# Routed tokens transposed by block exchange and VectorE in place of TensorE, and low weights made in two parts on two tiles

## The chip, the cores and the metric

The kernel runs on one core of a Trainium2 chip. The metric is device time in microseconds (us), the median of three runs of one launch. On the engines: PE (TensorE, with its weight loads as PEld), DVE (VectorE), ACT (ScalarE), POOL (GpSimd) and SP (SyncE, here an issuer of DMAs). Each engine has a sequencer that works through its instructions in order: waits, register loads from SBUF, branches and DMA issues are done there, and in rows they carry a q (PEldq).

## The reference, cut to what matters

A Mamba layer (a selective scan over 4 batches of 512 tokens) gated by the normed x is added to x; then a mixture of experts is added to that:

```python
x = x + tanh(g_xattn[0]) * mamba(ctx_1024, layernorm(x), ...)
h = layernorm(x)                              # 2048 tokens x 512
scores = softmax(h @ gate_w.T)                # 16 experts
topk_w, topk_ids = top_k(scores, 6)           # then made to sum to 1, as combine
for e in range(16):                           # hidden size I = 352
    g, u = split(h @ w13[e].T); acc += combine[:, e] * ((silu(g) * u) @ w2[e].T)
out = acc + shared(h)                         # the same form, hidden size 2 * 352
x = x + tanh(g_ffn[0]) * out
```

All of it is float32.

## The kernel before, in words

The first third of the span is stage A, the scan. Behind it stand 136 tiles of 128 tokens each (TILES). Tiles 0 to 31 (NS = 32) are the shared part, twice the 16 token tiles, with the shared weights as two sets; tiles 32 to 135 are routed. Each expert's tokens are listed and cut into tiles of 128, and a table in SBUF, `meta`, holds for each tile its expert, where its weights lie, whether it is the first or the last of an expert, and its column in the lists. Engines read it by register loads (`value_load`), since the plan depends on the data.

A matmul in single precision is made of three: each operand is split into a rounded high part and the low rest, and high x high, high x low and low x high are added. So a tile needs x_high (ACT, L852) and x_low (DVE, L1363); PE's `up`, 24 matmuls (L1699, L1700); ACT's silu and DVE's `multiply`; PE's `turn_a`, three transposes (L1710); ACT's a_high (L862) and DVE's a_low (L1399); PE's `down`, nine matmuls (L1719); ACT's y_out (L868); and POOL's add into the output, an indirect DMA with accumulation (L1015). PE's order in tile t is: half of up(t), turn_a(t - 1), the other half, turn_x(t + 1), down(t - 1), so that ACT and DVE have time between.

Routed x comes to its tile by POOL's indirect gather (L997) of 128 rows of `rows_d`, a table in DRAM of all tokens' rows with their routing weights behind; it is issued five tiles ahead (AHEAD) into `xt`, with four slots. A gathered tile has tokens on partitions, and `up` wants features there, so PE transposes it in four 128x128 pieces into bank 4 (turn_x, L1687), from which x_high and x_low read. DVE copies the routing weights of a tile (take_weight, L1372) and the row numbers of gather and add (L1378, L1383), each behind a register load (L1369, L1375).

Weights of an expert are one DMA of 2176 KB into `wraw`, issued by SP (L633). ACT (L822) and DVE (L1417) cast half of the high parts each on the tile ahead of the expert's first, and POOL makes all the low parts with one subtraction (L987). `w` holds two experts, so that PE changes between them by an offset, which it loads for each tile (weights_of, L1724 and L1726).

The order on each engine is written out: shared tiles and the first routed ones are unrolled, and from there each engine has a loop of four tiles. `apart` is a semaphore wait with a register's value. SP stores the rows of a batch into `rows_d` (L609) as soon as they are normed.

Of the kernel before, what the change touches and what calls it, by code (L numbers as in the profile page):

```python
# [64 lines left out]
AHEAD = 5  # L65
FIRST_ROWS = {NS - 3: (NS, NS + 1), NS - 2: (NS + 2,), NS - 1: (NS + 3, NS + 4)}
# [100 lines left out]
               8: [("exp", 3)], TT - 3: [("fetch", 2)]}  # L167
# [64 lines left out]
def mamba_moe(nc, x, ctxT, g_x, g_f, inT, convw, convb, xpT, dtwT, dtb, alog, dvec,  # L232
# [12 lines left out]
    with ExitStack() as ctx:  # L245
# [113 lines left out]
        wraw = alloc(ctx, "wraw", [P, WCOLS])  # L359
        w = alloc(ctx, "w", [P, 4 * WCOLS], F32R)  # L360
# [5 lines left out]
        cc = alloc(ctx, "cc", [P, 2])  # L366
# [8 lines left out]
        meta = alloc(ctx, "meta", [P, 5, NT], I32)  # L375
# [13 lines left out]
        fours = alloc(ctx, "fours", [P, 2], I32)  # L389
# [57 lines left out]
        gathered = [sem(f"gathered{i}") for i in range(4)]  # L447
        zero_done = sem("zero_done")
# [16 lines left out]
        cc_done = sem("cc_done")  # L465
# [42 lines left out]
        def routed_groups(eng):  # L508

            return eng.value_load(fours[0:1, 0:1], min_val=E // 4, max_val=ROUTED // 4)  # L510

# [29 lines left out]
        def _(sp):  # L541
# [42 lines left out]
            def step(b, at):  # L584
# [7 lines left out]
                if b == NB - 1 and n == 2:  # L592
                    sp.wait_ge(dA_done, b * DS * J)
                    sp.wait_ge(g_done, b * DS)
                    sp.wait_ge(summed, (b - 1) * DS * J + J * J)
                    fetch(0)
# [10 lines left out]
            def rows(b, _):  # L607
                sp.wait_ge(norm_done, TC * (b + 1))
                sp.dma_start(rows_v[b, :, :, 0:H + 2], rowb[:]).then_inc(rows_stored, 16)  # L609
# [20 lines left out]
            def fetch(e):  # L630

                at_least(sp, wl_done, e)
                sp.dma_start(wraw[:], wall[bass.ds(e, 1)].rearrange("a p c -> p (a c)")).then_inc(raw_in, 16)  # L633
# [24 lines left out]
            with sp.Fori(3, NX) as e:  # L658
                fetch(e)
            sp.wait_ge(meta_ready, 2)  # L660
            tiles = tiles_but_12(sp) + 12
# [5 lines left out]
        def _(act):  # L667
# [92 lines left out]
            def norm_chunk(b, t):  # L760
                act.wait_ge(nmr2_done, b + 1)
                act.wait_ge(rows_stored, 16 * (b + 1))
# [53 lines left out]
            def split_high(e, t):  # L816


                mine = WCOLS - SHARE
                apart(act, raw_in, 16 * (e + 1), "act")  # L820
                apart(act, down_done, t, "act")
                nc.scalar.copy(columns(w, (e % 2) * 2 * WCOLS, mine), wraw[:, 0:mine]).then_inc(wh_done, 1)  # L822
# [14 lines left out]
            def fetch(e):  # L837

                act.wait_ge(wl_done, e)
                act.dma_start(wraw[:], wall[bass.ds(e, 1)].rearrange("a p c -> p (a c)")).then_inc(raw_in, 16)  # L840
# [40 lines left out]
            def high_piece(e, k):  # L881
# [5 lines left out]
                nc.scalar.copy(w[:, base + at:base + at + size], wraw[:, at:at + size]).then_inc(*split(e, k, EARLY))  # L887
# [51 lines left out]
        def _(pool):  # L939
# [43 lines left out]
            def split_low(e):  # L983

                at = (e % 2) * 2 * WCOLS
                apart(pool, wh_done, 2 * (e + 1), "pool")
                nc.gpsimd.tensor_tensor(columns(w, at + WCOLS, WCOLS), wraw[:], columns(w, at, WCOLS), ALU.subtract).then_inc(wl_done, 1)  # L987

            def gather(t, s):

                if isinstance(t, int) and t < NS + 4:
                    pool.wait_ge(xl_done, t - 3)
                else:
                    apart(pool, xt_turned, t - 3, "pool")
                    apart(pool, cc_done, t - 3, "pool")
                apart(pool, gid_done, t + 1, "pool")
                pool.indirect_dma_start(xt[:, s, :], None, rows_d[:, :],  # L997
# [47 lines left out]
            for t in range(NS):  # L1045
                if t == NS - 3:
                    pool.wait_ge(wts_stored, 16 * NB)
                    pool.wait_ge(rows_stored, 16 * (NB + 1))
                for late in FIRST_ROWS.get(t, ()):
                    gather(late, late % 4)  # L1050
# [12 lines left out]
            with pool.Fori(0, groups - 2) as i:  # L1063
                for k in range(4):
                    t = 4 * i + NS + k
                    gather(t + AHEAD, (k + AHEAD) % 4)
# [4 lines left out]
            for k in range(8):  # L1071
                if k + AHEAD < 8:
                    gather(rest + k + AHEAD, (k + AHEAD) % 4)
# [6 lines left out]
        def _(dve):  # L1080
# [226 lines left out]
            def count_tiles(half):  # L1307

                if half:
# [5 lines left out]
                    chained(nc.vector.tensor_scalar(fours[:, 0:1], fours[:, 0:1], -float(NS // 4), None, ALU.add))  # L1315
                    return
# [26 lines left out]
            def fill_table(half):  # L1343
                if half == 0:
# [10 lines left out]
                                                       op0=ALU.is_lt, op1=ALU.mult))  # L1355
                nc.vector.scalar_tensor_tensor(out=meta[:, 2, :], in0=slot[:], scalar=1.0, in1=fresh[:],
# [8 lines left out]
            def take_weight(t, s4, m=None):  # L1365
# [3 lines left out]
                e = dve.value_load(meta[0:1, 0, bass.ds(t, 1)], min_val=1, max_val=NX)  # L1369
                rows_in(dve, t, s4, m, "dve")  # L1370
                at_least(dve, am_done, t - 1)
                nc.vector.tensor_copy(cc[:, s4 % 2:s4 % 2 + 1], xt[:, s4, bass.ds(H - 1 + e, 1)]).then_inc(cc_done, 1)  # L1372
# [4 lines left out]
            def gather_ids(t, s4):  # L1377
# [7 lines left out]
            def multiply(t, s):  # L1385
# [3 lines left out]
                else:  # L1389
                    dve.wait_ge(cc_done, t + 1)  # L1390
                    weight = cc[:, s:s + 1]
# [9 lines left out]
            def low_piece(e, k):  # L1401
# [4 lines left out]
                low = nc.vector.tensor_tensor(w[:, base + WCOLS + at:base + WCOLS + at + size], wraw[:, at:at + size],  # L1406
# [4 lines left out]
            def next_weights(t):  # L1411

                e = dve.value_load(meta[0:1, 2, bass.ds(t, 1)], min_val=0, max_val=NX - 1)
                with dve.If(e > 0):
                    apart(dve, raw_in, 16 * (e + 1), "dve")
# [405 lines left out]
```

## Time and profile before

| | |
|---|---|
| median of three runs | 1436.62 us (1435.21 to 1438.37) |
| the profiled execution: its span (the records show no time of its own beside it) | 1435.5 us |
| PE busy, of the span | 1349.9 us, 94% |
| POOL, DVE, ACT busy | 66%, 55%, 51% |
| DMA moved | 149.13 MB, mean 104 GB/s |
| granted TensorE clock, 720 to 1400 us | 1.00 (2.4 GHz) |

A busy share is a mean over stages; in the routed part DVE, ACT and POOL are far from full and PE nearly is. Matmuls' ends are modelled, so a busy PE need not be PE at its peak. An idle time is given with what ended it; "issue" is idle time that no wait in the profile explains, in which an engine's sequencer was still at something else.

### The profile page before, as it was taken

Reading aid. Unit: us, or ns where it says so; the run is one execution under the profiler, and the core shown is the slowest. Engines: PE = TensorE matmul, PEld = TensorE weight load, DVE = VectorE, ACT = ScalarE, POOL = GpSimd, SP = SyncE. Lnnn points to the kernel's source line nnn. Section 1 sums busy time; section 2 is a strip of 40 time slices with the busy share of each in tenths; the row PEclk is TensorE's granted clock in tenths of the full one; section 3 lists DMA queues with packets and bytes.
Section 4 is the critical chain, followed back from the end, with each engine's and each line's share of the span. In section 5 each row is a group of like instructions: output and inputs, shape, how many; then the busy total and the mean of one; then the engine's idle time right before and its main releaser. Section 6 shows DMA issues by size and latency. Waiting matters only on the chain.

```text
span 1435.5 us, 32257 instructions
## 1 busy us (share of the span) xinstructions
PE 1349.9 (94%) x8480; PEld 1210.6 (84%) x8481; DVE 787.5 (55%) x1364; ACT 730.9 (51%) x1317; POOL 949.3 (66%) x671
## 2 busy tenths in 40 slices
PE   6897998997898899999999999999999999999996
PEld 2686887887888799999998989989889988899885
DVE  6878898898989854653333333333333333333331
ACT  5898897898889464343332333323333333332321
POOL 0588898898988747887456665566645666546632
PEclk8899999999999999999999999999999999999999
DMA  4120122222242365645455435555445544454432
GB/s 137 38 74 31 53 67 96 67 73 91 75 146 72 133 129 106 142 84 141 83 141 145 131 63 144 139 147 137 104 94 137 141 135 104 95 147 131 76 68 36
DMA packets 65042, 149.13 MB, mean 104 GB/s; under 512 B 16976, under 2 KB 17616, under 8 KB 62656
## 3 DMA queue, kind: packets, MB, share of 16 engines
q0 software_dynamic: 31024, 62.10, 22.9%
q1 hardware_dynamic: 33392, 81.21, 17.5%
q10 hardware_dynamic: 560, 4.98, 1.0%
q8 instruction: 36, 0.59, 0.2%
q14 instruction: 30, 0.25, 0.1%
HBM read 101.50 MB, written 48.99 MB: 105 GB/s over the span
## 4 chain that ended last, share of the span: by engine, by line
PE 65%; DVE 3%; issue 1%; POOL 0%; ACT 0%; DVEq 0%; POOLq 0%; ACTq 0%
PE bank L1719 19%; PE bank L1699 19%; PE bank L1700 18%; PE bank L1687 3%; PE bank L1710 3%; DVE hs L1172 1%; PE bank L1604 1%; PE bank L1590 1%; PE bank L1602 0%; POOL hc L949 0%; DVE sc L1226 0%; PE bank L1665 0%; DVEq L1375 0%; DVE xl L1363 0%; DVE du L1186 0%
## 5 line engine op out<-in xcount | busy, mean ns | idle before, releaser
L949 POOL TENSOR_TENSOR hc<-hs,crow 128x512 f32<-128x512 f32 x254 | 322.6, 1302 | 91.8 <-DVE hs L1172 84.6
L1699 PE MATMUL bank<-w,xh 128*128 (+1 forms) x1088 | 368.7, 340 | 7.6 <-issue 4.2
L1015 POOL DMA_INDIRECT out_x<-ys,aid x104 | 171.2, 1646 | 275.0 <-issue 215.7
L1700 PE MATMUL bank<-w,xh 128*128 (+1 forms) x1088 | 351.2, 323 | 0.0
L1172 DVE TENSOR_TENSOR_SCAN hs<-dA,bank 128x512 f32<-128x512 f32 x256 | 295.8, 1208 | 47.9 <-PE bank L1604 32.0
L1719 PE MATMUL bank<-w,ah 128*128 (+1 forms) x816 | 264.7, 405 | 2.7 <-DVE al L1399 2.7
L1399 DVE TENSOR_TENSOR al<-bank,ah 128x384 fp32r<-128x384 f32 x136 | 75.8, 557 | 331.0 <-ACT ah L862 283.2
L1699 PEld LDWEIGHTS bank<-w,xh 128*128 128x128 f32 x1088 | 204.3, 188 | 35.9 <-issue 32.1
L1700 PEld LDWEIGHTS bank<-w,xh 128*128 128x128 f32 x1088 | 206.4, 190 | 2.3
L868 ACT COPY ys<-bank 128x512 f32<-128x512 f32 x136 | 79.9, 587 | 195.9 <-PE bank L1719 191.5
L1700 PE MATMUL bank<-w,xl 128*128 (+1 forms) x544 | 175.9, 323 | 0.0
L1699 PE MATMUL bank<-w,xl 128*128 (+1 forms) x544 | 175.7, 323 | 0.0
L1719 PEld LDWEIGHTS bank<-w,ah 128*128 128x128 f32 x816 | 145.0, 189 | 27.7 <-issue 2.2
L1590 PE MATMUL bank<-ident,hc 128*128 128x128 f32 x1024 | 160.4, 281 | 7.6 <-POOL hc L949 5.1
L862 ACT CAST ah<-bank 128x384 fp32r<-128x384 f32 x136 | 65.3, 480 | 196.9 <-PE bank L1710 166.7
L786 ACT ACTIVATE dA<-delta,aneg 128x512 f32<-128x512 f32 x256 | 164.0, 710 | 0.0
L1604 PE MATMUL bank<-bdiag,duT 128*128 128x128 f32 x1024 | 163.7, 285 | 0.0
L1719 PE MATMUL bank<-w,al 128*128 (+1 forms) x408 | 161.2, 395 | 0.0
L852 ACT CAST xh<-bank 128x512 fp32r<-128x512 f32 x104 | 61.2, 588 | 182.9 <-PE bank L1687 175.4
L987 POOL TENSOR_TENSOR w<-wraw,w 128x4352 f32 x15 | 143.8, 9588 | 0.7 <-issue 0.5
L1604 PEld LDWEIGHTS bank<-bdiag,duT 128*128 128x128 f32 x1024 | 142.5, 201 | 0.0
L1590 PEld LDWEIGHTS bank<-ident,hc 128*128 128x128 f32 x1024 | 124.3, 145 | 11.0 <-POOL hc L949 6.7
(184 smaller groups left out, 2051.7 us busy)
## 6 DMA issues: line engine op xcount, KB each, us to landing
wraw<-in_wall SPq DMA_DIRECT2D x16, 2176.0 KB
crow<-c_rows SPq DMA_DIRECT2D x64, 256.0 KB, 3.3
xt<-token_rows_turned SPq DMA_DIRECT2D x32, 256.0 KB
out_x<-ys POOLq DMA_DIRECT2D x32, 256.0 KB
wraw<-in_wall ACTq DMA_DIRECT2D x2, 2176.0 KB
token_rows<-rowb SPq DMA_DIRECT2D x4, 1028.0 KB
xrow<-in_x SPq DMA_DIRECT2D x4, 1024.0 KB, 7.0
out_x<-xrow SPq DMA_DIRECT2D x4, 1024.0 KB, 4.9
```

The source lines that it names most:

```text
L786: nc.scalar.activation(dA[:, 4 * (n % 2) + j, :], delta[b % 2][:, j, :], ACT.Exp, scale=aneg[:, j, n:n + 1]).then_inc(dA_done, 1)
L868: nc.scalar.copy(ys[:, slot, :], banks[7][:]).then_inc(ys_done, 1)
L949: nc.gpsimd.tensor_tensor(hc[:, j, :], hs[:, j, :], crow[:, n % 4, :], ALU.mult).then_inc(hc_done, 1)
L987: nc.gpsimd.tensor_tensor(columns(w, at + WCOLS, WCOLS), wraw[:], columns(w, at, WCOLS), ALU.subtract).then_inc(wl_done, 1)
L1015: pool.indirect_dma_start(out_rows, bass.IndirectOffsetOnAxis(ap=aid[:, s:s + 1], axis=0), ys[:, s, :], None, bounds_check=TOKENS - 1, oob ...
L1172: nc.vector.tensor_tensor_scan(hs[:, j, :], dA[:, 4 * (n % 2) + j, :], dbu[j % 2][:], 0.0, ALU.mult, ALU.add).then_inc(scanned, 1)
L1399: nc.vector.tensor_tensor(al[:, s, :], banks[5][:, 0:IP], ah[:, s, :], ALU.subtract).then_inc(al_done, 1)
L1590: mm = nc.tensor.matmul(ysum[t][:, cols], hc[:, j, t * P:(t + 1) * P], ident[:], start=n == 0 and j == 0, stop=n == DS - 1, is_transpose=T ...
L1604: mm = nc.tensor.matmul(dbu[j % 2][:, t * P:(t + 1) * P], duT[b % 2][:, t, j * P:(j + 1) * P], bdiag[:, n % 2, t - COPIED, :], start=True, ...
L1699: nc.tensor.matmul(gate_bank[:, 0:I], xx, columns(w, off + ww + k * 2 * I, I), start=first, stop=last)
L1700: mm = nc.tensor.matmul(up_bank[:, 0:I], xx, columns(w, off + ww + k * 2 * I + I, I), start=first, stop=last)
L1719: mm = nc.tensor.matmul(banks[7][:], aa, columns(w, off + ww + W2AT + k * H, H), start=k == 0 and n == 0, stop=k == IK - 1 and n == 2)
```

## The change

- `turn_x` is gone from PE. SP exchanges blocks instead: a gathered pair of tiles (`rowg`, four slots) is copied by 16 DMAs, each 32 partitions x 2 tiles x 512 bytes, so that block (q, c) of 32 partitions goes to block (c, q) of `xq` (part of `wraw`). DVE's `turn`, one instruction that transposes within 32x32 blocks, writes the whole turned tile into bank 4, at the start of DVE's tile, ahead of a_low. So that this is a transposition, a row's columns are stored in `rows_d` in another order: SP's store becomes 17 DMAs a batch in place of one.
- Gathers go out eight tiles ahead in place of five, row numbers seven, and routing weights three in place of one. The first row numbers are copied at tile 28 (with the wait for the lists), not 29.
- SP no longer fetches weights. ACT issues the fetch, at the last tile of an expert by a new column of `meta`, into `wnext` with two buffers, one expert further ahead.
- POOL makes the low weights in two instructions of half the width, the first on the tile it was on, the second on the next, by another column of `meta`: one more register load a tile on POOL, and one on ACT.

The diff, cut to its core:

```diff
+QUAD = P // 32
+AHEAD = 8
+TAKEN = 3
+FIRST_IDS = {NS - 4: (NS, NS + 1, NS + 2, NS + 3), NS - 2: (NS + 4, NS + 5), NS - 1: (NS + 6,)}
...
+            def exchange(i, h):
+                for k in (2 * h, 2 * h + 1):
+                    apart(sp, gathered[k], 16 * i + 16, "sp")
+                apart(sp, xt_turned, 4 * i + NS + 2 * h - 2, "sp")
+                for q in range(QUAD):
+                    for c in range(QUAD):
+                        sp.dma_start(xq[32 * c:32 * c + 32, 2 * h:2 * h + 2, q * P:(q + 1) * P],
+                                     rowg[32 * q:32 * q + 32, 2 * h:2 * h + 2, c * P:(c + 1) * P]).then_inc(swapped[h], 16)
...
+                last = act.value_load(meta[0:1, 5, bass.ds(t, 1)], min_val=0, max_val=NX - 2)
+                with act.If(last > 0):
+                    apart(act, wl_done, last, "act")
+                    fetch(last + 1)
...
-            def gather(t, s):
+            def gather(t, s, m):
+                if not (isinstance(m, int) and m == 0):
+                    apart(pool, swapped[s // 2], 16 * QUAD * QUAD * m, "pool")
                     apart(pool, cc_done, t - 3, "pool")
                 apart(pool, gid_done, t + 1, "pool")
...
+                before = pool.value_load(meta[0:1, 6, bass.ds(t, 1)], min_val=0, max_val=NX - 1)
+                with pool.If(before > 0):
+                    split_low(before, 1)
                 e = pool.value_load(meta[0:1, 2, bass.ds(t, 1)], min_val=0, max_val=NX - 1)
                 with pool.If(e > 0):
-                    split_low(e)
+                    split_low(e, 0)
...
+            def turn(t, s4, m):
+                apart(dve, swapped[s4 // 2], 16 * QUAD * QUAD * (m + 1), "dve")
+                dve.wait_ge(xh_done, t)
+                dve.wait_ge(xl_done, t)
+                nc.vector.transpose(banks[4][:].rearrange("p (k q j) -> p q k j", k=HK, q=QUAD),
+                                    xq[:, s4, :].rearrange("p (q k i) -> p q k i", q=QUAD, k=HK)).then_inc(xt_turned, 1)
...
+            def tile(t, s4, m=0, gathers=False, takes=False, adds=False):
+                turn(t + 1, (s4 + 1) % 4, m + (s4 + 1) // 4)
                 a_low(t - 1, 1 - s)
...
                 up(t, s, (2, 3), off)
-                if more and not (isinstance(t, int) and t + 1 < NS):
-                    turn_x(t + 1, (s4 + 1) % 4, m)
                 down(t - 1, 1 - s, old() if callable(old) else old)
```

On PE, before, in the routed loop, from the end of up to the register loads of the next tile:

```order
L1700 MATMUL bank<-w,xl 128x352
L1687 MATMUL bank<-ident,xt 128x128 [waits gathered1,xl_done]
L1687 MATMUL bank<-ident,xt 128x128 x3
L1719 ISA [waits ys_done,al_done]
L1719 MATMUL bank<-w,ah 128x512
...
L1719 MATMUL bank<-w,al 128x512
L1724 ISA
L1724 TENSOR_LOAD meta
```

The same place after (at the end of a group of four, so with the loop's branch):

```order
L1772 MATMUL bank<-w,xl 128x352
L1791 ISA [waits ys_done,al_done]
L1791 MATMUL bank<-w,ah 128x512
...
L1791 MATMUL bank<-w,al 128x512
L1828 REGISTER_ALU
L1828 COMPARE_AND_BRANCH
...
L1796 TENSOR_LOAD meta
```

The transposes and their waits are gone; the register load still stands behind all of down.

On DVE, before, the start of a routed tile:

```order
L1399 TENSOR_TENSOR al<-bank,ah 128x384 [waits down_done,ah_done]
L1369 ISA
L1369 TENSOR_LOAD meta
L1369 ISA x2
L1372 ISA [waits gathered1,am_done]
L1372 COPY cc<-xt 128x1
```

After:

```order
L1436 STREAM_TRANSPOSE bank<-wraw 128x4x4x32 [waits swapped0,xl_done,xh_done]
L1468 TENSOR_TENSOR al<-bank,ah 128x384 [waits down_done,ah_done]
L1424 ISA
L1424 TENSOR_LOAD meta
L1424 ISA x2
L1427 ISA [waits gathered3,am_done]
L1427 COPY cc<-rowg 128x1
```

The turn stands ahead of a_low, with its wait for the exchange (`swapped0`).

On POOL, before, a routed tile from its gather to its add:

```order
L997 DMA xt<-token_rows,gid 128x532 [waits gid_done]
L1032 ISA
L1032 TENSOR_LOAD meta
...
L987 TENSOR_TENSOR w<-wraw,w 128x4352
L1033 UNCONDITIONAL_BRANCH
L1038 ISA
L1038 TENSOR_LOAD meta
...
L1015 DMA out_x<-ys,aid 2048x512 [waits ys_done,aid_done]
```

After:

```order
L497 REGISTER_ALU [waits swapped0]
L497 REGISTER_ALU [waits cc_done]
L1045 DMA rowg<-token_rows,gid 128x532 [waits gid_done]
L1080 ISA
L1080 TENSOR_LOAD meta
...
L1035 TENSOR_TENSOR w<-wnext,w 128x2176
...
L1083 TENSOR_LOAD meta
...
L1035 TENSOR_TENSOR w<-wnext,w 128x2176
...
L1089 TENSOR_LOAD meta
```

The gather waits for the exchange, and three register loads stand where two did.

## Rows read from the trace of the kernel before

**Rows 1.** Page: busy us, share and count; two groups: busy, mean ns.

```profile
PE 1349.9 (94%) x8480; PEld 1210.6 (84%) x8481; DVE 787.5 (55%) x1364; ACT 730.9 (51%) x1317; POOL 949.3 (66%) x671
...
L1172 DVE TENSOR_TENSOR_SCAN hs<-dA,bank 128x512 f32<-128x512 f32 x256 | 295.8, 1208 | 47.9 <-PE bank L1604 32.0
...
L987 POOL TENSOR_TENSOR w<-wraw,w 128x4352 f32 x15 | 143.8, 9588 | 0.7 <-issue 0.5
```

**Rows 2.** Windows: us, then PE, PEld, DVE, ACT, POOL busy; clock, DMA share, GB/s.

```profile
720.00:1400.00 680.00, 673.70 (x3931) 612.66 (x3930) 241.73 (x603) 225.53 (x407) 394.83 (x212) 1.00 0.49 120
```

**Rows 3.** Chain of waits from 720 to 1400 us, by line.

```profile
by line: PE bank L1719 29.4%; PE bank L1699 29.1%; PE bank L1700 27.5%; PE bank L1687 6.1%; PE bank L1710 4.7%; issue 1.8%; DVEq L1375 0.4%; DVE xl L1363 0.3%; DVEq L1369 0.2%; ACT ah L862 0.2%; ACTq L872 0.1%; DVEq L487 0.0%; DVE al L1399 
```

**Rows 4.** Page, costliest groups: weight loads of L1699; behind the bar, idle before.

```profile
L1699 PEld LDWEIGHTS bank<-w,xh 128*128 128x128 f32 x1088 | 204.3, 188 | 35.9 <-issue 32.1
```

**Rows 5.** Timeline of weight loads at tile starts: start us, us, instruction, [idle before].

```profile
899.93 0.19 PEld L1699 LDWEIGHTS bank<-w,xh 128*128 128x128 f32 x1
...
906.67 0.19 PEld L1699 LDWEIGHTS bank<-w,xh 128*128 128x128 f32 x1
...
1003.45 0.19 PEld L1699 LDWEIGHTS bank<-w,xh 128*128 128x128 f32 x1 [0.18 <-issue]
...
1010.48 0.19 PEld L1699 LDWEIGHTS bank<-w,xh 128*128 128x128 f32 x1 [0.45 <-issue]
...
1017.18 0.19 PEld L1699 LDWEIGHTS bank<-w,xh 128*128 128x128 f32 x1
```

**Rows 6.** Timeline of DVE, a_low and the gather ids.

```profile
1006.54 0.56 DVE L1399 TENSOR_TENSOR al<-bank,ah 128x384 fp32r<-128x384 f32 x1 [2.24 <-ACT ah L862]
...
1008.52 0.15 DVE L1378 COPY gid<-lists 128x1 int32 x1 [0.86 <-issue]
...
1021.25 0.56 DVE L1399 TENSOR_TENSOR al<-bank,ah 128x384 fp32r<-128x384 f32 x1 [1.23 <-ACT ah L862]
```

**Rows 7.** Register loads of L1724: ns min/median/max, first and last start us.

```profile
L1724 PEldq TENSOR_LOAD <-meta x103: 296/385/1000, 703.9 to 1411.3; - x103
...
L1724 PEldq TENSOR_LOAD <-meta x1: 897/897/897, 1008.0 to 1008.0; - x1
...
L1724 PEldq TENSOR_LOAD <-meta x1: 298/298/298, 1023.1 to 1023.1; - x1
```

**Rows 8.** Timeline of POOL, adds.

```profile
1005.61 1.59 POOL L1015 DMA_INDIRECT out_x<-ys,aid  x1 [4.11 <-issue]
...
1019.35 2.13 POOL L1015 DMA_INDIRECT out_x<-ys,aid  x1 [4.12 <-ACT ys L868]
```

**Rows 9.** Timeline of ACT, y_out of tile 31 and of tile 134.

```profile
706.65 0.59 ACT L868 COPY ys<-bank 128x512 f32<-128x512 f32 x1 [1.38 <-PE bank L1719]
...
1419.97 0.59 ACT L868 COPY ys<-bank 128x512 f32<-128x512 f32 x1 [1.79 <-PE bank L1719]
```

**Rows 10.** DVE by line, 900 to 1400 us: busy, mean ns, idle before, releasers.

```profile
L1363 DVE TENSOR_TENSOR xl<-bank,xh 128x512 fp32r<-128x512 f32 x72 | 49.8, 692 | 15.6 <-ACT xh L852 14.4
...
L1399 DVE TENSOR_TENSOR al<-bank,ah 128x384 fp32r<-128x384 f32 x72 | 40.1, 557 | 171.2 <-ACT ah L862 148.7 <-issue 22.5
```

**Rows 11.** Timeline of SP's queue, two DMA issues one behind the other.

```profile
24.61 0.43 SPq L628 DMA_DIRECT2D ids<-in_ids_d  x1
25.09 0.43 SPq L628 DMA_DIRECT2D tri<-in_tri_d  x1
```

**Rows 12.** Timelines at 676 to 685 us, and the lists' DMA (KB, us to landing).

```profile
676.40 0.56 DVE L1399 TENSOR_TENSOR al<-bank,ah 128x384 fp32r<-128x384 f32 x1 [3.79 <-issue]
...
677.62 0.63 PE L1719 MATMUL bank<-w,ah 128*128 128x512 f32 x2
...
678.11 0.59 POOL L1060 DMA_DIRECT2D lists<-token_lists  x1 [0.47 <-DMA token_lists<-ids,posi]
...
lists<-token_lists POOLq DMA_DIRECT2D x1, 136.0 KB, 3.8
...
684.58 0.15 DVE L1378 COPY gid<-lists 128x1 int32 x1 [0.60 <-issue]
```

More of the change, by code:

```diff
@@ L447, in mamba_moe @@
         gathered = [sem(f"gathered{i}") for i in range(4)]
+        swapped = [sem(f"swapped{i}") for i in range(2)]
+        cc_done = sem("cc_done")
         zero_done = sem("zero_done")
@@ L608, in rows @@
                 sp.wait_ge(norm_done, TC * (b + 1))
-                sp.dma_start(rows_v[b, :, :, 0:H + 2], rowb[:]).then_inc(rows_stored, 16)
+                with nc.allow_non_contiguous_dma(reason="a row's columns by quadrant of the transposed row"):
+                    for t in range(TC):
+                        for c in range(QUAD):
+                            sp.dma_start(rows_v[b, :, t, c * P:(c + 1) * P].rearrange("p (k i) -> p k i", k=HK),
+                                         rowb[:, t, 0:H].rearrange("p (k c i) -> p c k i", k=HK, c=QUAD)[:, c]).then_inc(rows_stored, 16)
+                    sp.dma_start(rows_v[b, :, :, H:H + 2], rowb[:, :, H:H + 2]).then_inc(rows_stored, 16)
             def turned_(b, _):
@@ L657, in _ @@
                 x_load(t)
-            with sp.Fori(3, NX) as e:
-                fetch(e)
-            sp.wait_ge(meta_ready, 2)
+            def exchange(i, h):
[3 more added lines that the diff above has]
+                for q in range(QUAD):
+                    for c in range(QUAD):
+                        sp.dma_start(xq[32 * c:32 * c + 32, 2 * h:2 * h + 2, q * P:(q + 1) * P],
+                                     rowg[32 * q:32 * q + 32, 2 * h:2 * h + 2, c * P:(c + 1) * P]).then_inc(swapped[h], 16)
+            sp.wait_ge(meta_ready, 2)
+            sp.wait_ge(wl_done, 2)
+            groups = routed_groups(sp)
+            with sp.Fori(0, groups) as i:
+                for h in range(2):
+                    exchange(i, h)
             tiles = tiles_but_12(sp) + 12
@@ L1489, in _ @@
             groups = routed_groups(dve)
-            tile(PEELED, PEELED % 4)
+            tile(PEELED, PEELED % 4, -1)
             next_weights(PEELED)
-            for k in range(1, 4):
-                tile(PEELED + k, (PEELED + k) % 4, True, True)
-                next_weights(PEELED + k)
-            with dve.Fori(0, groups - 1) as i:
+            for t in range(NS, NS + 3):
+                tile(t, t % 4, 0, gathers=True, takes=True, adds=True)
+                next_weights(t)
+            most = groups_but_2(dve)
+            with dve.Fori(0, most) as i:
                 for k in range(4):
                     t = 4 * i + NS + 3 + k
-                    tile(t, (3 + k) % 4, True, True, i + 1)
+                    tile(t, (3 + k) % 4, i + (3 + k) // 4, gathers=True, takes=True, adds=True)
                     next_weights(t)
-            last = tiles_but_12(dve) + 11
-            a_low(last - 1, 0)
-            add_ids(last, 3)
-            multiply(last, 1)
-            a_low(last, 1)
+            rest = tiles_but_12(dve) + 7
+            for k in range(4):
+                tile(rest + k, (3 + k) % 4, most + (3 + k) // 4, takes=k < 2, adds=True)
+                next_weights(rest + k)
+            a_low(rest + 3, 0)
+            add_ids(rest + 4, 3)
+            multiply(rest + 4, 3, most + 1)
+            a_low(rest + 4, 1)
         @block.tensor
@@ L1681, in beside @@
                         last_count(i)
-            def turn_x(t, s, m=None):
-                rows_in(pe, t, s, m, "pe")
-                at_least(pe, xl_done, t)
-                for k in range(HK):
-                    mm = nc.tensor.transpose(banks[4][:, k * P:(k + 1) * P], xt[:, s, k * P:(k + 1) * P], ident[:])
-                mm.then_inc(xt_turned, 1)
             def up(t, s, chunks, off):
@@ L1726, in weights_of, with tile @@
                 return pe.value_load(meta[0:1, 1, bass.ds(t, 1)], min_val=0, max_val=2 * WCOLS)
-            def tile(t, s4, old, off, more=True, m=None):
+            def tile(t, s4, old, off):
                 s = s4 % 2
@@ L1764, in _ @@
                     off = weights_of(4 * i + PEELED + k)
-                    tile(4 * i + PEELED + k, (3 + k) % 4, old, off, True, i)
+                    tile(4 * i + PEELED + k, (3 + k) % 4, old, off)
                     old = off
@@ L1770, in of_last @@
                 return pe.value_load(meta[0:1, 1, bass.ds(last - k, 1)], min_val=0, max_val=2 * WCOLS)
-            tile(last, 3, lambda: of_last(1), weights_of(last), False)
+            tile(last, 3, lambda: of_last(1), weights_of(last))
             turn_a(last, 1)
```

129 lines of the change are left out of this document (77 added, 52 removed).

## The prediction

> **What bounds the kernel now.** I read the page's busy shares first, then the table of windows, the chain of waits, the costliest groups, and the timelines of single tiles. Two statements about the routed part are both true and lead to different forecasts. PE is busy 94% of the span [rows 1] and 673.7 of 680 us between 720 and 1400 us [rows 2], and the chain of that stretch is nearly all matmuls, 6.1% of it the x transposes of L1687 [rows 3]: 41.5 us for 98 tiles, 0.42 a tile. Read alone, that says: take 104 x 0.42 us away and the time falls by as much. But the ends of matmuls are modelled, and the weight loads tell another story: ahead of L1699, PEld stood idle 35.9 us in all, 32.1 of it put down to issue [rows 4]. Something holds PE's sequencer at the start of many tiles while the array has nothing to do.
>
> The timeline of one tile shows it. It begins with its first weight load at 1003.45, and the next at 1010.48, after 0.45 us of idle [rows 5]: 7.03 us. VectorE's a_low (L1399), which the down matmuls need, ends at 1006.54 + 0.56 = 1007.10 [rows 6], 3.65 after the start. The sequencer is held at the first down matmul until then, issues the nine, and only then reaches the register load of the next tile's weights (L1724), which starts at 1008.0, 0.90 later, and takes 0.897 [rows 7]. From its end at 1008.90 to the next tile's start lie 1.58 us, in which the second load (L1726) stands. 3.65 + 0.90 + 0.90 + 1.58 = 7.03: the tile is this chain, and the x transposes are not in it.
>
> The load is not always so long: 103 of them took 0.296 at least, 0.385 in the median, 1.000 at most [rows 7], and 0.485 as the mean that I work out over the 103. The long ones follow the add of a finished tile (L1015): add at 1005.61 [rows 8], load at 1008.0, 2.4 behind it, ended 3.3 behind it. Where the add lay further back, at 1019.35 [rows 8], 3.75 ahead of the load at 1023.1, the load took 0.298 [rows 7]. In the loads that I looked at, those that start 2 to 3 us behind an add end about 3.3 behind it, and others are short. I call them held.
>
> Without a held load the chain has 3.64 + 0.92 + 0.30 + 1.53 = 6.39 us, each the value that its piece has in most of the 103 tiles. Every fourth tile has 0.40 more at the loop's end (a_low's end at 1021.25 + 0.56, [rows 6], the load at 1023.1: 1.3 in place of 0.9): 6.49 in the mean. Where no load is held the array decides: 899.93 to 906.67, 6.74, without issue idle at either end [rows 5]. So now a tile takes the longer of the two.
>
> From the y_out of tile 31 at 706.65 to the next to last at 1419.97 [rows 9] are 103 tiles in 713.3 us, 6.93 each. 15 of them change the expert (15 low-weight instructions, [rows 1]); there the casts stand ahead of a_high and a_low, as in the tile from 1017.18 [rows 5], whose a_low ends at 1021.81, 4.63 after the start. That is 0.9 more than elsewhere in the mean of nine that I read, and 0.13 over all tiles. The chain's account of now: 6.49 + 0.19 held + 0.13 casts = 6.81; the 0.12 that is missing to 6.93 is what the array adds where it is the longer one.
>
> **The change, part by part.**
>
> *The transposes go from PE.* The array's floor falls to 6.74 - 0.42 = 6.3, below the chain's 6.49. What is late next is therefore the chain alone: if loads are held as now and the casts stay, 6.81 against 6.93, 0.12 x 103 = 12 us gained.
>
> The Trainium skill bears on the price of the load. On the page DMA: Bandwidth & Descriptors, section Latency and other measured facts, it gives tensor_load a floor of about 600 ns. By that the chain would have 0.3 more than it has here, the array's fall would bring nothing, and the sum would be 12 us higher. The measured 0.296 decides, and the sum does not use the page.
>
> *VectorE's turn comes in.* One 128x512 transpose per tile, ahead of a_low. No row shows one: the nearest are x_low, 0.692 on the same shape [rows 10], and the scan, 1.208 [rows 1]; I take 0.7. In 72 tiles a_low waited 171.2 us, 148.7 of it for ScalarE's a_high [rows 10], 2.1 a tile: either end fits in. Cost 0; if the turn came late and that cover were gone, each 0.1 us is 10 us. x_high and x_low are ready earlier, off the chain: no gain.
>
> *The exchange on SP.* Sixteen DMAs for a pair of tiles. SP's issues stand 0.48 us apart (24.61, 25.09, [rows 11]), and a load of 136 KB landed 3.8 after issue [rows 12]: 16 x 0.48 + 3.8 = 11.5 us, against 13.8 for two tiles, and it starts a tile and a half before the pair is over. It reads and writes 0.5 MB more in 13.8 us, 38 GB/s. The 16 DMA engines are busy 0.49 of the time at 120 GB/s [rows 2]; by bytes that is 0.16 more. Cost 0; the bound above is a pair that takes longer than two tiles, a rival below. The stores of the rows, 17 in place of one for each batch, lie beside a scan that doesn't wait for them: 0.
>
> *Weights earlier and issued by ScalarE; low weights in halves.* PE does not wait for low weights (9.59 us, [rows 1], against six or seven tiles between experts); two parts of 4.8 change nothing there. ScalarE gets one more load and branch a tile, an estimated 0.8 us on an engine busy a third of the time [rows 2]: 0. But POOL's gather, now for tile t + 8 where it was t + 5, waits for gather ids that VectorE copies a tile later, and POOL's register loads, three where there were two, stand behind it and ahead of the add. The ids end 5.2 after a tile's start (1008.52 + 0.15, [rows 6]). The gather's issue and three loads with their branches, estimated by VectorE's 0.75 from one load's copy to the next [rows 12], make 8.2, and the add 1.0 behind them comes 9.2 after that start, 2.5 after the next one; now it is 2.16 (1005.61 - 1003.45). PE's first load, 4.56 after the start, is then 2.06 behind the add, at the edge of the stretch in which it is held; in even tiles, in which the gather also waits for the exchange, it lies elsewhere. Bounds: no load held, 0, or one held in full in each tile, 0.70. I take as much as now, 0.19.
>
> *The start of the routed part.* VectorE now waits for the token lists ahead of tile 28 in place of tile 29. The lists' DMA is issued at 678.11 and lands 3.8 later, at 681.9, where a_low of tile 27 ran at 676.40 [rows 12]. Behind the wait stands that a_low, and PE's down matmuls, now at 677.62 [rows 12], wait for it: a_low ends at 682.5, and PE loses about 5.0. Then four gather-id copies stand ahead of x_low, where there were two, 0.15 + 0.60 each (684.58, [rows 12]): 1.5 more. With 1 us for the four operations added at tile 20 and the three takes at tile 31: 7.5 us lost. The bounds are 0, if the lists came 5 us earlier, and 12.
>
> **Sum.** On the profiled execution: 1435.5 - 12 + 7.5 = 1431.0. The records show its span only, which is 1.1 below the median of the three timed runs, 1436.6. So 1432 us, 0.3% less.
>
> **Rivals.**
>
> *The array is the bound.* For it: 99% busy, and the chain of waits [rows 2, 3]. Against it: 32.1 us of issue idle [rows 4] and the sum of 7.03. It gives 44 less and 7.5 more: 1400.
>
> *No load is held any more.* For it: the moved add is near the edge, and PE's load may miss the stretch in most tiles. Against: the add moves differently in even tiles. 0.12 + 0.19 = 0.31 x 103 = 32: 1436.6 - 32 + 7.5 = 1412.
>
> *Slower: a load is held in each tile.* The moved add puts one of PE's two loads, of L1724 or of L1726, into the stretch in every tile. For it: the tile shown, held 0.6 us, and two loads that can be hit; against: while POOL makes low weights no add is out, and that is now in two tiles of each six or seven. 6.49 + 0.70 + 0.13 = 7.32: 0.39 x 103 = 40 and 7.5, 1484; if it holds half of the tiles, 6.97, 1448. It decides from 0.24 us of holding a tile on, where the gain falls below the 7.5 of the start.
>
> *Slower: the exchange sets the pace.* It does so from 13.8 / 16 = 0.86 us per DMA on. At 1.0 a pair takes 16 us: 2.2 x 52 = 114 us, 1558. Against: issues 0.48 apart [rows 11], if their landings overlap.
>
> In the Trainium skill the page DMA: Bandwidth & Descriptors, section Rules for kernel authors, speaks for this one: many small transfers should be made one, since under 64 KB one pays mostly overhead; a DMA of the exchange has 32 KB. The trace shows small loads issued one behind the other without such a pause.
>
> **Chances.** The forecast, the chain with loads held about as now: 0.45, with its own range of 1422 to 1443. Array 0.10; no load held 0.17; a load held in each or in half of the tiles 0.22; exchange 0.06. A measurement of this kernel tells 0.2%, 2.9 us, from no change. Faster: 0.10 + 0.17 and 0.21 of the forecast's, 0.48; same: 0.15 of the forecast's and 0.03 of the half-held case, 0.18; slower: 0.19 + 0.06 and 0.09 of the forecast's, 0.34. The range leaves out the fully held case, the exchange, and the lower edge of the array's: 1397 to 1460.
>
> **What would show it.** If the chain bounds, PE's matmul share falls below 94% and issue idle ahead of L1699's weight loads rises above the 32.1 us; if the array did, it falls. Register loads on PE's sequencer keep a median near 0.385, or not. One gap of about 5 us stands on PE near 677, with a_low behind the lists. The turn takes 0.7 to 1.2 us and ends ahead of a_high. The forecast is wrong if tiles run at 6.3 (array), if VectorE's turn is what a_low waits for, or if the turn waits for the exchange.

## The result and the profile after

The changed kernel takes 1463.3 us (median of 4 runs, 1462.0 to 1465.6) against 1437.5 of the kernel before in the same call: ratio 1.0181, 95% interval 1.0167 to 1.0196. It is slower by 26 us, 3 us above the range.

The page of the changed kernel: busy shares, the queue that SP and its exchange use, and the weight loads of a tile's first half (behind the bar, idle before).

```profile
PE 1331.1 (91%) x8064; PEld 1167.0 (80%) x8065; DVE 854.2 (58%) x1471; ACT 732.2 (50%) x1317; POOL 954.3 (65%) x686
...
q1 hardware_dynamic: 131584, 75.11, 22.8%
...
L1771 PEld LDWEIGHTS bank<-w,xh 128*128 128x128 f32 x1088 | 204.3, 188 | 76.4 <-issue 73.5
```

The queue has 131,584 packets, four times the 33,392 of before. PE is at 91% where it was at 94% [rows 1], and issue idle ahead of the first weight loads is 73.5 us where it was 32.1 [rows 4]: taking work from the array did not make the tiles shorter. The same window and the chain of waits (720 to 1420 us) say what took its place.

```profile
720.00:1400.00 680.00, 636.27 (x3464) 556.65 (x3463) 300.30 (x688) 223.57 (x401) 400.48 (x223) 1.00 0.65 156
```

```profile
by line: issue 15.9%; PE bank L1791 13.7%; PE bank L1771 13.1%; PE bank L1772 11.8%; SPq L688 10.0%; DMA wraw<-rowg 9.1%; DMA rowg<-token_rows,gid 3.5%; PE bank L1782 2.2%; POOLq L1080 2.2%; DMA out_x<-ys,aid 2.1%; POOLq L1083 2.0%; POOLq L
```

PE's share of this chain falls from nearly all [rows 3] to some 41%, and the issues and landings of the exchange (L688, `wraw<-rowg`) and the gathers stand in it. From y_out to y_out (ScalarE's timeline; first the last y_out of the kernel before, tile 135, then tiles 31, 134 and 135 of the changed one):

```profile
1424.66 0.59 ACT L868 COPY ys<-bank 128x512 f32<-128x512 f32 x1 [3.35 <-PE bank L1719]
```

```profile
717.05 0.59 ACT L908 COPY ys<-bank 128x512 f32<-128x512 f32 x1 [1.87 <-PE bank L1791]
...
1443.31 0.59 ACT L908 COPY ys<-bank 128x512 f32<-128x512 f32 x1 [1.79 <-PE bank L1791]
1449.83 0.59 ACT L908 COPY ys<-bank 128x512 f32<-128x512 f32 x1 [4.42 <-PE bank L1791]
```

Tile 31 ends 10.4 us later than before (706.65, [rows 9]), 10.6 when counted from the first y_out of each kernel. The 104 tiles behind it take 732.8 us, 7.05 each, where they took 718.0. 10.6 + 14.8 is the change of the span, 1460.7 - 1435.5, but for 0.2.

**The ring of row slots.** The four slots of `rowg` go round: a pair is gathered, lands, is issued to the exchange, lands there, and only then may POOL gather the pair four tiles on. One turn on the timelines of SP (issues) and POOL (gathers, adds):

```profile
975.83 0.60 SPq L688 DMA_DIRECT2D wraw<-rowg  x1
...
1004.67 0.60 SPq L688 DMA_DIRECT2D wraw<-rowg  x1
```

```profile
990.81 1.93 POOL L1045 DMA_INDIRECT rowg<-token_rows,gid  x1 [5.41 <-issue]
994.18 1.59 POOL L1063 DMA_INDIRECT out_x<-ys,aid  x1 [1.43 <-issue]
996.08 0.99 POOL L1045 DMA_INDIRECT rowg<-token_rows,gid  x1 [0.30 <-issue]
```

The pair's issues begin at 975.83 and take 10.3; 4.7 later, at 990.81, the first row gather of the next round starts; the second one, behind an add, at 996.08, 5.3 later; 8.6 later its rows have landed and the next exchange on the same slots begins, at 1004.67: 28.8 us for four tiles. The mean of 48 such turns is 28.3: 10.6 of issues, 5.9 to the first gather, 5.9 to the second, 5.9 to the next issue. That is 7.07 a tile, which is what the tiles took; but whatever goes round with the tiles has their pace, so the sum alone does not show that the ring sets it. What speaks for it is that in the turn shown each part ends in a wait for the next: SP for the rows of a gather, POOL for the DMAs of an exchange. The waits over the routed part agree (the first row is SP's: us in total, times, longest; the second says who waited for the exchange's DMAs, us and times):

```profile
SPq L505 <- DMA rowg<-token_rows,gid: 132.0, 42, 9.4
```

```profile
  POOL rowg L1045: 141.1, 27
```

It reaches PE by way of VectorE. POOL's adds stand behind those gathers: they start 9.6 us behind the end of their y_out in the mean, 2.3 before. VectorE's add_ids for the tile four on waits for them, with multiply behind it and PE's turn_a behind that. VectorE's and PE's timelines: the first row waits for the add of 994.18; in the second and third, two tiles on, 4.86 us of POOL's low weights stood ahead of the add as well.

```profile
1004.24 0.15 DVE L1451 COPY aid<-lists 128x1 int32 x1 [2.07 <-DMA out_x<-ys,aid]
...
1020.51 0.15 DVE L1451 COPY aid<-lists 128x1 int32 x1 [4.09 <-issue]
```

```profile
1021.28 0.55 PE L1782 MATMUL bank<-ident,am 128*128 128x128 f32 x3 [1.57 <-DVE am L1462]
```

**The start.** Timelines at the lists: ScalarE's fetch of weights, POOL's store of the lists, VectorE's a_low and PE's down of tile 27 (one fence for each engine).

```profile
674.21 0.35 ACTq L880 DMA_DIRECT2D wnext<-in_wall  x1
```

```profile
682.47 0.59 POOL L1111 DMA_DIRECT2D lists<-token_lists  x1 [4.33 <-DMA token_lists<-ids,posi]
```

```profile
685.06 0.56 DVE L1468 TENSOR_TENSOR al<-bank,ah 128x384 fp32r<-128x384 f32 x1 [11.93 <-DMA lists<-token_lists]
```

```profile
685.67 1.22 PE L1791 MATMUL bank<-w,ah 128*128 128x512 f32 x2 [7.36 <-DVE al L1468]
```

a_low waits for the lists as forecast, but the lists go out at 682.47, not 678.11 [rows 12]: the last token lists land some 4 us later, beside a fetch of 2176 KB that the change put there. Behind the wait PE was slower, too: from the first of down's nine matmuls, at 685.67, to the next tile's first, at 689.54, lie 3.9 us, where it was 2.1 before (677.62 to 679.71). The granted clock was 1.00 from 675 to 682 us and 0.57 in the mean from 682 to 690, for most of it at the lower level, 1.2 GHz: it fell while PE stood idle for 7.4 us, and was back at 1.00 (2.4 GHz) from 690. Windows of the kernel before and of the changed one (columns as in [rows 2]):

```profile
680.00:720.00 40.00, 39.53 (x231) 36.20 (x230) 13.65 (x34) 14.03 (x25) 19.75 (x12) 1.00 0.43 79
```

```profile
680.00:720.00 40.00, 33.02 (x174) 29.50 (x175) 13.94 (x32) 10.37 (x18) 13.94 (x14) 0.91 0.56 130
```

### The profile page after: what moved, and what is told of

Read it like the earlier page. It is cut to its first block, busy times and chain, and to the rows that moved or that the text cites. A ratio compares the mean times of both kernels' runs of the same rounds, so it can differ in the third digit from the quotient of the medians.

```text
span 1460.7 us, 34077 instructions
## 1 busy us (share of the span) xinstructions
PE 1331.1 (91%) x8064; PEld 1167.0 (80%) x8065; DVE 854.2 (58%) x1471; ACT 732.2 (50%) x1317; POOL 954.3 (65%) x686
## 3 DMA queue, kind: packets, MB, share of 16 engines
q1 hardware_dynamic: 131584, 75.11, 22.8%
## 4 chain that ended last, share of the span: by engine, by line
PE 31%; issue 10%; DMA 8%; SPq 7%; POOL 5%; POOLq 4%; DVE 3%; ACT 2%; DVEq 1%; ACTq 1%
PE bank L1791 10%; PE bank L1771 9%; PE bank L1772 8%; SPq L688 7%; DMA wraw<-rowg 4%; POOL token_lists L1075 3%; DMA rowg<-token_rows,gid 2%; PE bank L1782 1%; DVE hs L1221 1%; POOLq L1080 1%; DMA out_x<-ys,aid 1%; POOLq L1083 1%; PE bank L1683 1%; PE bank L1669 1%; POOLq L1089 1%
## 5 line engine op out<-in xcount | busy, mean ns | idle before, releaser
L1791 PE MATMUL bank<-w,ah 128*128 (+1 forms) x816 | 260.8, 401 | 16.8 <-DVE al L1468 16.4
L1771 PEld LDWEIGHTS bank<-w,xh 128*128 128x128 f32 x1088 | 204.3, 188 | 76.4 <-issue 73.5
L1063 POOL DMA_INDIRECT out_x<-ys,aid x104 | 166.5, 1601 | 138.5 <-issue 64.8
L1045 POOL DMA_INDIRECT rowg<-token_rows,gid x104 | 109.3, 1051 | 187.3 <-issue 163.0
L1791 PEld LDWEIGHTS bank<-w,ah 128*128 128x128 f32 x816 | 150.1, 190 | 47.8 <-issue 15.2
L1035 POOL TENSOR_TENSOR w<-wnext,w x30 | 146.4, 4881 | 8.1 <-issue 7.7
```

Of the source, the lines that this page charges most:

```text
L1035: low = nc.gpsimd.tensor_tensor(columns(w, at + WCOLS, size), columns(raw, source + half * size, size), columns(w, at, size), ALU.subtract)
L1045: pool.indirect_dma_start(rowg[:, s, :], None, rows_d[:, :], bass.IndirectOffsetOnAxis(ap=gid[:, s:s + 1], axis=0)).then_inc(gathered[s], 16)
L1063: pool.indirect_dma_start(out_rows, bass.IndirectOffsetOnAxis(ap=aid[:, s:s + 1], axis=0), ys[:, s, :], None, bounds_check=TOKENS - 1, oob ...
L1771: nc.tensor.matmul(gate_bank[:, 0:I], xx, columns(w, off + ww + k * 2 * I, I), start=first, stop=last)
L1791: mm = nc.tensor.matmul(banks[7][:], aa, columns(w, off + ww + W2AT + k * H, H), start=k == 0 and n == 0, stop=k == IK - 1 and n == 2)
```

## The experiments

Times are medians of four executions (ten for POOL's order by pairs); ratios are to the kernel before, with 95% intervals. Differences to the changed kernel compare two such ratios, so one of 3 or 4 us needs the trace beside it. "Routed part" is y_out of tile 31 to y_out of tile 135: 718.0 us before, 732.8 after.

**The exchange as one DMA.**

```diff
-                for q in range(QUAD):
-                    for c in range(QUAD):
-                        sp.dma_start(xq[32 * c:32 * c + 32, 2 * h:2 * h + 2, q * P:(q + 1) * P],
-                                     rowg[32 * q:32 * q + 32, 2 * h:2 * h + 2, c * P:(c + 1) * P]).then_inc(swapped[h], 16)
+                sp.dma_start(xq[:, 2 * h:2 * h + 2, :], rowg[:, 2 * h:2 * h + 2, 0:H]).then_inc(swapped[h], 16)
...
```

The two waits for the exchange, not shown, count one DMA in place of sixteen. The kernel leaves out the transposition of routed x.

> The changed kernel, with the sixteen DMAs of a pair's exchange replaced by one DMA of the same bytes that moves no block to another place (so the routed part of the result is left out of account: x is not transposed). Theory 'ring': the four row slots go round gather, landing, 16 issues (10.6 us), landing, next gather, in 28.3 us per four tiles, 7.07 a tile, and the routed tiles ran at 7.05; without the issues the ring has some 18 us and stops deciding, so tiles fall to PE's chain, 6.5 to 6.7: about 1463 - 40 = 1423 us. Rival 'traffic': the bytes that the exchange adds to the DMA engines (share 0.49 to 0.65) make it late; they stay, so 1450 or more. Rival 'POOL': the third register load and the later gather ids move the adds, whatever the exchange costs: 1455 to 1463.

1448.3 us, ratio 1.0082 (1.0065 to 1.0099); routed part 713.8. The direction is as expected, the size is not: 15 us for 40, in the total nearer to what "traffic" gave than to the ring's 1423. POOL hardly waits for the exchange (3 us in all), but 6.9 us still lie between the gathers of a pair, adds start 3.8 us behind their y_out, and a tile takes 6.86. PE's longest waits are issue idle at the start of a tile, 19.5 us, and x_low, 11.6 (720 to 1400 us).

**A quarter of the bytes** in sixteen DMAs (`c * P:c * P + 32`, and so for q); three quarters of routed x are left out.

> The changed kernel with its sixteen DMAs per pair, each moving a quarter of its bytes (32 of 128 columns; three quarters of x are left out). 'Ring': the 10.6 us of issues stay and only landings beside a weight fetch get shorter, 28.3 to about 27 us: 1445 to 1460. 'Traffic': three quarters of the added bytes are gone: 1430 or less.

1455.4 us, 1.0132 (1.0103 to 1.0160). Fewer bytes bring 8 us, one issue in place of sixteen 15: the number of DMAs counts for more than their bytes, and "traffic", 1430 or less, is out.

**POOL's order by pairs**, the exchange as it is.

```diff
-                    gather(t + AHEAD, (k + AHEAD) % 4, i + (k + AHEAD) // 4)
                     next_weights(t)
                     expert_starts(t, k)
                     add(t, k)
+                    for late in (k - 1, k) if k % 2 else ():
+                        gather(4 * i + NS + late + AHEAD, late % 4, i + (late + AHEAD) // 4)
```

> The changed kernel, with POOL's order per pair of tiles: both tiles' low weights and adds first, then both gathers. Theory 'ring': the 5.9 us from one gather of a pair to the other fall to about 1.3, so the ring of four row slots takes some 24 us in place of 28.3 and no longer decides, and adds are no longer held by gathers that wait for an exchange, so add_ids doesn't wait for them: tiles at or under the 6.86 of the one-DMA exchange, 1463 - 20 = 1443 (1436 to 1450). Rival 'traffic' or 'landing': the exchange's landing decides, and the order of POOL changes nothing, 1460 or more.

1438.2 us, ratio 1.0004 (0.9994 to 1.0014): 25 us of 26 are gone, with each DMA of the exchange in place. The routed part is 707.9, 10 less than before the change. The two gathers of a pair are 1.3 apart, as expected (POOL's timeline). They no longer wait for the exchange (five adds do, 10.5 us in all, as in the first row), and the adds wait for y_out again (last row: us in total, times, longest): they start 1.0 us behind its end in the median, where it was 9.3:

```profile
1003.70 1.59 POOL L1063 DMA_INDIRECT out_x<-ys,aid  x1 [1.74 <-DMA wraw<-rowg]
1005.59 1.01 POOL L1045 DMA_INDIRECT rowg<-token_rows,gid  x1 [0.30 <-issue]
1006.91 0.98 POOL L1045 DMA_INDIRECT rowg<-token_rows,gid  x1 [0.30 <-issue]
```

```profile
POOL out_x L1063 <- ACT ys L908: 128.1, 27, 5.9
```

The edit does two things at once: it shortens the ring by some 4.6 us, and it takes the adds out from behind the wait. One DMA shortens the ring and leaves POOL's order, and gave 19 of these 25 us in the routed part. How the 25 divide between the two, no run says.

**Low weights in one part again** (`split_low(e)` over all of WCOLS, the load of `meta[6]` gone).

> The changed kernel with the low weights in one part of 9.6 us again, on the first tile alone. Theory 'ring': POOL's 4.85 us parts stand between the two gathers of a pair (8.8 us where 5.2 are usual) or ahead of the first; one part of 9.6 stands in one turn of the ring where two of 4.85 stood in one or two, about the same sum, but all in one place, so the adds of that tile are 4.8 us later: 1463 to 1472. Rival: the split costs by itself (a third register load a tile ahead of each add): 1450 or less.

1489.0 us, 1.0368 (1.0339 to 1.0397), 26 more than the changed kernel, far above the expected 0 to 9. In the ring a part of 9.6 us holds an add, and through add_ids the tile (POOL, then VectorE):

```profile
735.73 9.61 POOL L1033 TENSOR_TENSOR w<-wnext,w  x1
745.51 1.62 POOL L1059 DMA_INDIRECT out_x<-ys,aid  x1 [0.18 <-issue]
```

```profile
751.23 0.15 DVE L1444 COPY aid<-lists 128x1 int32 x1 [6.58 <-DMA out_x<-ys,aid]
```

Eight tiles of 12 to 14 us stand there, and PE waits 40 us for multiply in all. With these stalls the mean granted clock fell to 0.95 from 720 to 1000 us and to 0.98 from 1000 to 1400, where it was 1.00 in the changed kernel, so part of the 26 is the clock. The split, priced at 0, is worth 26 us in this kernel, though PE never waits for low weights.

**Three quarters of the transposes away**, from the kernel before (`for k in range(1)` in turn_x; three quarters of routed x are left out).

> The kernel before with one of the four x transposes of a routed tile on PE (three quarters of x are left out). The prediction's term by itself: if PE's sequencer chain bounds, three quarters of 12 us are gained, 1437 - 9 = 1428. If the array bounds, 0.32 us x 104 tiles = 33: 1404.

1422.9 us, 0.9907 (0.9891 to 0.9924): 13.5 us less, between the two and nearer to the chain's 9 than to the array's 33. A tile takes 6.77 in the mean.

**PE's register loads ahead of down**, from the kernel before; three tiles of four, then all four (the core of the second form).

```diff
...
                     turn_x(t + 1, (s4 + 1) % 4, m)
+                if ahead:
+                    later = weights_of(t + 1)
                 down(t - 1, 1 - s, old() if callable(old) else old)
...
```

> The kernel before, with the register loads of the next tile's weights put ahead of down in three tiles of four, where PE's sequencer waits for a_low anyway. If the chain behind a_low bounds, those tiles fall from 6.93 to the array's 6.74: 0.15 x 78 = 12 us less, 1425. If the array bounds: 1437, no change.

1442.5 us, 1.0045 (1.0028 to 1.0061): slower, where 12 us less were expected. Most tiles fell to 6.73 or 6.74, as expected, but one in four took 7.55 in the mean: at the loop's start three loads came ahead of its down, one of them (L1726) at times held, up to 0.97 us. Hence the second form, with the offsets kept in registers over the loop's end:

> The kernel before, with the register loads of the next tile's weights ahead of down in all four tiles of the loop, kept in registers over the loop's end (in the trial with three of four, the fourth tile took 7.26 to 7.97 since three loads stood ahead of its down). If PE's chain behind a_low bounds, nearly all tiles take the array's 6.74, those with a cast 7.2: 104 x 6.82 = 709 for 718, about 1427 us (1423 to 1431). If the array bounds: 1436.

1425.9 us, 0.9921 (0.9905 to 0.9938), as expected; routed part 705.3. Issue idle ahead of L1699 is 11.9 us for 32.1 [rows 4]:

```profile
L1699 PEld LDWEIGHTS bank<-w,xh 128*128 128x128 f32 x1088 | 204.5, 188 | 17.4 <-issue 11.9
```

The loads behind a_low were what held most tiles, and without them the array with its transposes does.

**The start.** The wait for the lists and the first copies behind multiply:

> The changed kernel, with the wait for the token lists and the first copies of row numbers and routing weights behind multiply of their tiles, not ahead of a_low and x_low. Theory: of the 10.6 us that the shared part lost, most is a_low of tile 27 behind that wait (11.9 us of idle on VectorE, 7.4 on PE); it goes, and what stays is that the first exchange can't be ready before some 702 us: 1463 - 7 = 1456 (1452 to 1460). Rival: the loss is only moved to the first turn, 1463.

1462.5 us, 1.0183 (1.0166 to 1.0200): the rival's time. PE's wait for a_low only moved: it is 7.6 us one tile later, and 2.1 us more in the tile of the first turn, which waits for the exchange (PE's waits from 672 to 720 us: us in total, times, longest; VectorE's timeline):

```profile
PE bank L1793 <- DVE al L1468: 9.7, 2, 7.6
```

```profile
706.15 0.73 DVE L1436 STREAM_TRANSPOSE bank<-wraw 128x512 f32<-128x512 f32 x1 [5.25 <-DMA wraw<-rowg]
```

The fetch at tile 18 (`TT + 2: [("fetch", 3)]` for `NS - 5: [("fetch", 3)]`):

> The changed kernel with one edit: ACT issues the fetch of the fourth set of weights at tile 18, not at tile 27. In the changed kernel that fetch (2176 KB, issued at 674.21) stands beside the last token lists, whose landing took 4.3 us of wait where it took 0.5 before, and the lists' DMA went out at 682.47 for 678.11. Theory: those 4.4 us are the part of the start that the prediction did not have (10.6 for 7.5): 1463 - 4 = 1459 (1457 to 1461). Rival: the later gathers and exchange decide the start anyway, as they did when the wait was moved: 1462 to 1464.

1458.1 us, 1.0155 (1.0135 to 1.0174), an interval that touches the changed kernel's. The trace decides: the lists go out without that wait (POOL), and the shared part loses 7.4 us, not 10.6 (in the traces with this start unchanged it loses 10.6 to 12.6):

```profile
676.33 0.59 POOL L1111 DMA_DIRECT2D lists<-token_lists  x1 [0.45 <-DMA token_lists<-ids,posi]
```

**Edits together.** POOL's order and PE's loads, on the changed kernel:

> The changed kernel with two edits: POOL's order by pairs (which alone gave 1438) and PE's register loads ahead of down in all tiles. If PE's chain behind a_low is what is left after the ring, the tiles of 6.81 fall by 0.3 or more, x_low behind the copies of weights and row numbers being late next: 1438 - 25 = 1413 (1405 to 1425). If not: 1435.

1428.1 us, 0.9933 (0.9917 to 0.9950), 9.5 us less than before, where 25 were expected: routed part 697.8. PE's waits there are for a_low, 9.6 us, and x_low, 5.4.

Those two, the wait behind multiply, and x_low straight behind a_low (copies of weights and row numbers behind multiply):

> The changed kernel with the late start removed, POOL's order by pairs, PE's register loads ahead of down in all tiles, and on VectorE x_low straight behind a_low, with the copies of routing weights and row numbers behind multiply. If ring and chain are what bound, tiles come near to the array's 6.3 without the transposes, 6.4 to 6.6 with casts: 104 x 6.5 = 676 for 733, and 7 us at the start: about 1400 (1390 to 1420), faster than both. If the exchange's landings or its traffic bound, 1440 or more.

1419.8 us, 0.9883 (0.9866 to 0.9899), at the upper edge of what was expected. The median tile is 6.34 and many take 6.29, the array's time without transposes; expert tiles take 7 to 8.

In addition turn behind a_low everywhere, and the first wait in tile 29:

> The kernel with all four edits of the run before it, and two more on VectorE: turn stands behind a_low, not ahead of it, and the first wait for the lists stands in tile 29 behind a_low. In that run PE waited 25 us for a_low, which stood behind turns that waited 32 us for an exchange, and the shared part lost 10 us. Theory: a late exchange now delays only x_high and x_low, which have 2 us to spare: 1420 - 20 - 8 = 1392 (1385 to 1402). Rival: the exchange itself is too late, then x_low takes the place of a_low as PE's wait: 1412 or more.

1422.4 us, 0.9904 (0.9879 to 0.9928): no gain where 28 us were expected. The turns' wait for the exchange is gone (1.6 us in all, 38.8 in the run before), and PE still waits 23 us for a_low, so a turn behind a late exchange was not what made that wait. I had read it wrongly. Most of the tiles over 7.2 us are those of the expert changes, whose casts stand ahead of a_high.

The four edits of 1419.8, with the first wait in tile 29 behind a_low, turn behind a_low in tile 31 only, and the fetch at tile 18:

> The run with all four edits (1420), with that fetch at tile 18, the first wait for the lists in tile 29 behind a_low, and in tile 31 alone turn behind a_low. Theory: its shared part, 213.3 us for 203.4 of the kernel before, loses 7 of its 10 us: 1413 (1409 to 1416), the fastest of all. Rival: the first exchange ends at 703 us whatever comes ahead of it: 1418 or more.

1416.0 us, 0.9861 (0.9845 to 0.9878): the lowest of all, 1.4% under the kernel before, though the interval overlaps that of 1419.8. Of the 10 us in the shared part it takes back 3.7, not the 7 expected. Its weight loads:

```profile
L1780 PEld LDWEIGHTS bank<-w,xh 128*128 128x128 f32 x1088 | 205.1, 189 | 14.9 <-issue 6.3
```

## Why the prediction was wrong

**The step that failed is "The exchange on SP ... Cost 0".** It compared one exchange, 11.5 us, with two tiles, 13.8, and named a pair that takes longer than two tiles as the only way in which it could cost. The issues took 10.6 us where 7.7 were forecast, and 4.5 in the median, or 7 to 10 where a weight fetch had just gone out or POOL's low weights stood in between, lay between the last issue and the next gather. More than that, the exchange is one part of a ring through four slots, and the ring's other parts were never added: exchange, landing, two gathers in POOL's order, landing. In the prediction's own numbers that is 11.5, a tile of 6.9 until the second gather, and a landing of rows that it did not look up (median 4.8, up to 8.3, in the changed kernel's trace): some 23 of the 27.6 us of four tiles, and with the issues and landings as they were, 28.3. There was no tile and a half to spare. POOL's order by pairs takes 25 us back with the exchange untouched, so what cost them is the ring and POOL's place in it, not the exchange by itself; one DMA in place of sixteen, with POOL untouched, takes 15 back.

**The step on POOL looked for the wrong effect.** It asked where the add comes against PE's register loads, at 2.5 us after a tile's start, and took the wait for the exchange in even tiles as a detail. That wait moved the adds to 9.6 us behind their y_out, and they came back through add_ids, multiply and turn_a, a path that the prediction does not name. The holding of PE's loads got no worse, as forecast: the two loads of a tile (L1796, L1798) take 0.78 us together in the mean, 0.79 before.

**The transposes' term, 12 us, was about right.** With POOL's order by pairs the routed part is 10 us shorter than before, 6.81 a tile, the chain's forecast; three quarters of the transposes alone bring 13.5. That the array was not what bound a tile is shown by the earlier loads, 12 us with every transpose in place. Of the 44 us of the rival 29 come, and only when chain, ring and VectorE's order are changed together: the routed part of the fastest version is 688.6.

**The start: 7.5 forecast, 10.6 measured.** The mechanism was right, and two terms were missing. One is a landing slowed by a transfer that the change had moved there: PE waits 7.4 us for a_low where 5.0 were forecast. The prediction priced that move at 0 by ScalarE's time alone. The other is the clock: 1.8 us of the loss are matmuls at the lower level behind that wait. Without the fetch beside the token lists the loss is 7.4, but of other parts than forecast, 4.5 of waiting and 1.6 of clock (its nine matmuls take 3.7) among them; that it meets the 7.5 is in part luck.

**Turn** takes 0.726 us for the 0.7 taken, and waits for the exchange 10 us in all, nine times from 720 to 1400 us: it fits in, as forecast.

So the forecast's two terms at their measured sizes, -10 and +10.6, give 1438 (measured 1438.2 with POOL's order by pairs), and the 25 us that stand above it had no term. The rival on the exchange had the right place and a wrong threshold, 0.86 us per DMA: at the measured 0.66 the exchange already held POOL.

The Trainium skill, page DMA: Bandwidth & Descriptors, section Rules for kernel authors, would have small transfers coalesced; the one-DMA exchange agrees, 15 us faster, where a quarter of the bytes brought 8. But 25 us came without fewer DMAs.

## What to carry to other kernels

When a buffer ring gets a new stage, add the whole round: every wait, issue and landing from one use of a slot to its next, on all queues, and compare it with the tiles that the ring holds, not one stage with one tile. On an in-order queue, put what others wait for (here the adds) ahead of what may itself wait (the gathers). A busy engine with issue idle ahead of its tiles may be bound by its sequencer, as PE was here: move register loads to where it waits anyway before taking work from its array.

## What was not expected of the hardware

Issues of the exchange's DMAs on SP stand 0.66 us apart, where issues of constants stood 0.48 apart [rows 11]; some took up to 1.8 us. Beside a fetch of 2176 KB POOL waited 4.33 us for the landing of the last token lists, small indirect DMAs, and 0.45 with the fetch moved away. Register loads on PE are held behind an add as the prediction read it from a few: in the kernel before, 49 of the 51 loads of L1724 that start 2 to 3 us behind an add took over 0.45 us, and none of the others; in the changed kernel they reached 1.1. And where tiles of 12 to 14 us stand (low weights in one part), the granted clock falls for a while, though PE is 90% busy over the stretch:

```profile
720.00:1000.00 280.00, 250.81 (x1323) 222.43 (x1322) 115.77 (x266) 86.06 (x153) 153.41 (x80) 0.95 0.62 151
1000.00:1400.00 400.00, 372.33 (x2016) 330.54 (x2015) 175.90 (x399) 131.60 (x233) 222.16 (x120) 0.98 0.64 152
```

Left open: how much of the 26 us of the whole low weights is clock and how much stall. By these rows the clock took at most some 22 us of full-speed time (an estimate: 0.05 of 280 and 0.02 of 400), less where PE was waiting anyway.
